# Routed experts of L0_ffn and L3_ffn: token rows sent to the experts and results fetched back by indirect transfers

## The chip, the cores and the metric

One core of one Trainium2 chip runs the whole program. The time is the device time of one execution in microseconds; a median of several executions is given. Smaller is better.

## The reference, cut to what matters

The program is a stack of graph and feed-forward stages on 256 tokens of 768 columns, all in float32. L0_ffn and L3_ffn are mixtures of 8 experts with 2 chosen per token, and a shared expert that takes every token. This is their part of the computation as the kernel does it:

```
probs = softmax(x @ router)            # 8 logits per token; the two largest: w1, w2, divided by w1 + w2
for each expert e, for the tokens that chose it:
    h = silu(x @ gate[e]) * (x @ up[e])      # 768 -> 768 in L0_ffn, 768 -> 384 in L3_ffn
    out = out + weight * (h @ down[e])       # back to 768
out = out + shared expert(x) + the residual rows
```

In L0_ffn the weights are also scaled with a sigmoid gate between routed and shared experts, and L1_gnn follows with a normalization of each row. L3_ffn is the last stage; its rows are the output.

## The kernel before, in words

The program is written engine by engine: `sync_program`, `tensor_program`, `scalar_program`, `vector_program` and `gpsimd_program` call one function per stage, and what stands first in a function is issued first on that engine. Engines meet through semaphores, `mark` to signal and `at` to wait. Nothing reorders.

Weights stream from DRAM on SP's queue through `weight_ring`, five slots of 128 x 4608 float32 (2304 KB). `load` takes the slots in turn and first waits for `unit_free` of the unit that lay there. A gate, up or down matrix of an L0_ffn expert fills a slot each; in L3_ffn gate and up (1152 KB each) share one, and down (1152 KB) has one.

Each expert has 96 places for tokens (`NARROW`), split as 64 and 32 rows. The place of a token is counted on PE and DVE (`slots_pe`, `slots_dve`). If an expert gets more than 96, a flag is set and `taken_branch` runs a slow correction at the stage's end; every engine tests the flag there.

Token rows come to an expert by products. DVE's `select_dve` writes a 0/1 matrix S (256 tokens x 96 places) for each expert, and `pair_dispatch_pe` multiplies the normalized rows `xn_tok` with S for two experts at a time: 12 products, 24 rows of the trace, since the trace shows each float32 product as two. The results come back in the same manner: `weigh_dve` scales S with the token's weight, `weights_turn` turns it on PE, `cb_copy` brings it back, and `combine_A` (64 places of two experts) and `combine_B` (32 places of four) multiply expert outputs `outA`, `outB` with it and add onto banks 0 to 3. Those banks (`acc_tok`) hold the stage's sum from its beginning; `residual_pe` starts them with the residual rows.

Per expert PE does, in L0_ffn (`packed_pe`): gate, up (96 products on 32-column groups), then what `beside_silu_pe` names, the turning of the hidden rows (`packed_hidden_pe`), what `beside_copies_pe` names, and down (48 products). The two `beside` functions put dispatches and combines where ACT and DVE work on the hidden rows. In L3_ffn `both_experts_pe` does the same with half as many products. At the end `shared_down_pe` and the last combines finish the sum; L1_gnn's normalization, or the copies to `x_tok` and the two output transfers, follow.

## Time and profile before

| | |
|---|---|
| median of 3 runs | 1814.47 us (1813.79 to 1817.63) |
| the profiled execution's own time | 1809.26 us |
| its span | 1807.4 us |
| TensorE busy | 1711.3 us, 95% |
| VectorE, ScalarE, GpSimd busy | 624.7, 444.5, 26.4 us |
| mean granted clock | 0.991 |

The span runs from the first to the last instruction; the execution's own time has 1.9 us more around it. Line numbers are those of the kernel before. Matmul lines all have one number, 114, and transposes 117, so work is told by its tiles: `r_xd` is an expert's token rows, `r_hT` its turned hidden rows, `r_S` the selection, `r_cbA` and `r_cbB` the turned weights. L0_ffn's expert loop runs from 555.1 to 741.5 us, L3_ffn's from 1678.0 us to the end.

### The profile page before, as it was taken

How to read it: one execution, taken by the hardware profiler on the slowest of the kernel's cores; microseconds unless marked ns; L12 is line 12 of the kernel's file. 1: busy time of each engine (PE TensorE's matmuls, PEld its weight loads, DVE VectorE, ACT ScalarE, POOL GpSimd, SP SyncE). 2: the span in 40 equal slices, each digit the busy share in tenths (PEclk: the TensorE clock that was granted, in tenths of full speed). 3: DMA queues.
4: the chain of work that ended last, by engine and by line, in shares of the span. 5: the costliest groups of instructions: out<-in, count | busy, mean ns of one | idle time of the engine just before them, and what ended most of it. 6: DMA issues, size and time to landing. Idle time of an engine off the chain costs nothing.

```text
span 1807.4 us, 27462 instructions
## 1 busy us (share of the span) xinstructions
PE 1711.3 (95%) x12188; PEld 1021.6 (57%) x12188; DVE 624.7 (35%) x1178; ACT 444.5 (25%) x816; POOL 26.4 (1%) x35
## 2 busy tenths in 40 slices
PE   7999999999999999799999988887999999999998
PEld 4675445764466555477654433334575645767664
DVE  4415994049972221461420000002422422142331
ACT  0014883048841101341210000002511010131110
POOL 0000000000000000000000000000002000000000
PEclk9999999999999999889999999999999999999999
DMA  9205886139746877402589999999363164301661
GB/s 394 106 26 172 215 251 245 66 109 214 262 163 257 325 301 299 165 1 105 220 346 386 429 429 427 429 427 429 161 260 120 69 249 185 143 27 53 263 248 60
DMA packets 80749, 408.28 MB, mean 226 GB/s; under 512 B 9768, under 2 KB 50240, under 8 KB 58992
## 3 DMA queue, kind: packets, MB, share of 16 engines
q1 hardware_dynamic: 76112, 402.41, 58.6%
q10 hardware_dynamic: 4512, 4.03, 0.7%
q8 instruction: 100, 1.64, 0.4%
q14 instruction: 25, 0.20, 0.0%
HBM read 400.85 MB, written 5.51 MB: 225 GB/s over the span
## 4 chain that ended last, share of the span: by engine, by line
PE 80%; DMA 13%; DVE 4%; ACT 1%; issue 1%; SPq 0%; POOL 0%; DVEq 0%; ACTq 0%
PE banks L114 78%; DMA weight_ring<-in_L_ffn_c_fc_dram 8%; PE banks L117 2%; DMA weight_ring<-in_L_gnn_W_in_dram 2%; DMA weight_ring<-in_L_ffn_c_proj_e_dram 2%; DMA node_parts<-gate_node_parts 1%; DMA gate_rows<-node_parts 1%; DVE stat L273 1%; DVE weight_ring L120 0%; DVE xn_tok L125 0%; DMA ident<-in_c_ident_dram 0%; SPq L154 0%; DMA gate_queries<-in_L_gnn_query_rep_dram 0%; ACT weight_ring L148 0%; DVE xT L137 0%
## 5 line engine op out<-in xcount | busy, mean ns | idle before, releaser
L114 PE MATMUL banks<-weight_ring,xT 128*128 128x384 f32 x864 | 292.5, 490 | 1.5 <-DVE rgat_xr L137 1.5
L120 DVE TENSOR_TENSOR weight_ring<-weight_ring,gate_queries 128x1024 f32<-128x1024 f32 x192 | 222.8, 1222 | 17.5 <-ACT weight_ring L148 11.7
L114 PEld LDWEIGHTS banks<-weight_ring,xT 128*128 128x128 f32 x864 | 161.9, 191 | 107.9 <-issue 7.8
L148 ACT ACTIVATE weight_ring<-banks 128x1024 f32<-128x1024 f32 x192 | 191.0, 1024 | 42.8 <-PE banks L114 39.5
L114 PE MATMUL banks<-xT,weight_ring 128*128 128x256 f32 x792 | 178.2, 379 | 3.2 <-ACT x_tok L151 3.2
L114 PEld LDWEIGHTS banks<-xT,weight_ring 128*128 128x128 f32 x792 | 149.8, 190 | 27.4 <-issue 3.6
L114 PE MATMUL banks<-weight_ring,r_xd 128*32 128x384 f32 (+1 forms) x2304 | 142.7, 406 | 0.0
L114 PE MATMUL banks<-weight_ring,moe_xdT 128*64 128x384 f32 x720 | 122.0, 489 | 20.5 <-DMA weight_ring<-in_L_ffn_c_fc_dram 20.4
L114 PEld LDWEIGHTS banks<-weight_ring,r_xd 128*32 128x32 f32 x2304 | 76.7, 110 | 63.2 <-issue 54.9
L114 PE MATMUL banks<-gate_rows,selrow 96*128 96x512 bf16 x384 | 107.4, 381 | 3.1 <-ACT weight_ring L148 1.8
L114 PE MATMUL banks<-weight_ring,selrow 128*32 128x256 f32 x1536 | 102.0, 385 | 1.6 <-DVE weight_ring L120 1.5
L137 DVE COPY y_tok<-banks 128x384 f32<-128x384 f32 x32 | 17.8, 558 | 247.2 <-PE banks L117 247.2
L114 PEld LDWEIGHTS banks<-weight_ring,moe_xdT 128*64 128x64 f32 x720 | 49.9, 137 | 89.1 <-issue 57.9
L114 PE MATMUL banks<-weight_ring,y_tok 128*64 128x384 f32 x504 | 85.9, 490 | 10.5 <-DMA weight_ring<-in_L_ffn_c_proj_e_dram 10.5
L148 ACT ACTIVATE moe_h_tok<-banks 128x384 f32<-128x384 f32 x32 | 15.7, 491 | 265.9 <-PE banks L114 265.9
L114 PE MATMUL banks<-weight_ring,r_hT 128*32 128x192 f32 (+1 forms) x1152 | 73.2, 407 | 1.0 <-ACT r_hT L151 1.0
L114 PEld LDWEIGHTS banks<-weight_ring,selrow 128*32 128x32 f32 x1536 | 40.4, 109 | 58.2 <-issue 26.7
L114 PEld LDWEIGHTS banks<-weight_ring,y_tok 128*64 128x64 f32 x504 | 34.3, 137 | 55.1 <-issue 39.6
L114 PEld LDWEIGHTS banks<-gate_rows,selrow 96*128 96x128 bf16 x384 | 29.8, 97 | 59.6 <-issue 34.3
L114 PEld LDWEIGHTS banks<-weight_ring,r_hT 128*32 128x32 f32 x1152 | 36.7, 110 | 37.7 <-issue 34.4
L120 DVE TENSOR_TENSOR selrow<-banks,gate_node_parts 128x384 f32<-128x384 f32 x16 | 8.6, 555 | 129.8 <-ACT gate_node_parts L151 99.8
L120 DVE TENSOR_TENSOR r_h<-banks,r_silu 128x256 f32<-128x256 f32 (+2 forms) x32 | 13.3, 416 | 108.9 <-PE banks L114 77.3
(370 smaller groups left out, 1808.1 us busy)
## 6 DMA issues: line engine op xcount, KB each, us to landing
weight_ring<-in_L_ffn_c_fc_dram SPq DMA_DIRECT2D x30, 2304.0 KB, 23.0
weight_ring<-in_L_ffn_c_proj_e_dram SPq DMA_DIRECT2D x21, 2304.0 KB, 28.3
gate_queries<-in_L_gnn_query_rep_dram SPq DMA_DIRECT2D x48, 512.0 KB, 4.4
weight_slot_heads<-in_L_ffn_c_proj_e_dram SPq DMA_DIRECT2D x9, 2304.0 KB, 28.8
weight_ring<-in_L_ffn_w_gate_dram SPq DMA_DIRECT2D x8, 2304.0 KB, 10.0
weight_ring<-in_L_ffn_w_up_dram SPq DMA_DIRECT2D x8, 2304.0 KB, 8.9
weight_ring<-in_L_ffn_w_down_dram SPq DMA_DIRECT2D x8, 2304.0 KB, 9.7
weight_ring<-in_L_ffn_w_dram SPq DMA_DIRECT2D x16, 1152.0 KB, 8.0
```

Of the source, the lines that this page charges most:

```text
L114: return self.e.matmul(out, lhsT, rhs, start=start, stop=stop)
L117: return self.e.transpose(out, src, self.ident[0:n, 0:n])
L120: return self.e.tensor_tensor(out, a, b, op)
L137: return self.e.tensor_copy(out, a)
L148: return self.e.activation(out, a, f, **kw)
L273: t = v.e.bn_stats(half_stats[:, c, h, :], src[:, 2 * c + h, :])
```

## The change

- ACT clears a DRAM table `slot_rows` (768 x 768 float32, 2304 KB) early in L0_gnn, by a transfer from a constant.
- Experts 0 and 1 still get their rows by products. After that DVE (`index_dve`, 11 small operations) makes for each token the row numbers of its two places, and GpSimd (`send_pool`) writes the rows of `xn_tok` to `slot_rows` by four indirect transfers of 128 rows of 3 KB. For experts 2 to 7 SP loads 96 rows from the table (`slot_rows_sp`), and PE turns them with 6 transposes (`rows_turn_pe`); DVE and ACT copy half each (`expert_xd`).
- An expert's output goes by two SP transfers (64 and 32 rows) to a DRAM table `expert_rows` (`expert_rows_sp`). After the last, GpSimd (`fetch_pool`) reads each token's two rows with four indirect transfers into `chosen`, and DVE (`chosen_dve`) adds them with their weights onto `x_tok`. `weigh_dve`, `weights_turn`, `cb_copy` and the combines are gone.
- Banks 0 to 3 hold only the shared expert's sum, made at the end (`last_sums_pe`: 10 products in L0_ffn, 20 in L3_ffn). In L0_ffn `rows_added_pe` then adds `x_tok` with 4 products; in L3_ffn DVE adds the banks to `x_tok`, and `y3` to it in the loop. The 4 residual products at L0_ffn's beginning are gone; of those of L3_ffn two pairs became 3 small idle products each and two pairs are gone.
- PE begins the next expert's gate (in L3_ffn gate and up) before it turns the hidden rows, and finishes it after. Load order follows.
- Several semaphores are renamed; that is left out here.

```diff
+            a.dma(dram["slot_rows"], dram["c_zero"]).then_inc(*mark("slot_rows_zero", 0, 16))
...
+        def index_dve(v, B, v1, v2, z):
+
+            s, slot, mask, oh2, tm, row = B["stage"], B["slot"][:], B["sc"][1][:], *(x[:] for x in B["sc"][2:5])
+            both, second, w1, w2 = (B["pick"][:, i, :] for i in range(4))
+            v.then(v.ts(tm, slot, float(NARROW), ALU.is_ge, float(BEYOND), ALU.mult))
+            v.then(v.stt(row, bc(desc[:].unsqueeze(1), [P, TC, NEXP]), -float(NARROW), slot, ALU.mult, ALU.add))
+            v.then(v.tt(row, row, tm, ALU.add))
+            v.tt(tm, row, mask, ALU.mult)
+            v.then(v.tt(oh2, row, oh2, ALU.mult))
+            v.red(both, tm, ALU.add)
+            v.then(v.red(second, oh2, ALU.add))
+            v.tt(w1, v1, z, ALU.mult)
+            v.tt(w2, v2, z, ALU.mult)
+            v.stt(B["index"][:, 0, :], both, float(SLOTS), second, ALU.add, ALU.subtract)
+            v.ts(B["index"][:, 1, :], second, float(SLOTS), ALU.add).then_inc(*mark("index", s))
+
+        def send_pool(g, B):
+
+            s = B["stage"]
+            g.then(g.e.memset(B["chosen"][:], 0.0))
+            g.wait_ge(*at("slot_rows_zero"))
+            g.wait_ge(*at("index", s))
+            for c in range(TC):
+                for i in range(2):
+                    g.e.indirect_dma_start(
+                        out=dram["slot_rows"], out_offset=bass.IndirectOffsetOnAxis(ap=B["index"][:, i, c:c + 1], axis=0),
+                        in_=xn_tok[:, c, :], in_offset=None, bounds_check=SLOTS - 1, oob_is_err=False,
+                    ).then_inc(*mark("rows_sent", s, 16))
+
+        def fetch_pool(g, B):
+
+            s = B["stage"]
+            g.wait_ge(*at("expert_rows_0", (s, NEXP - 2)))
+            g.wait_ge(*at("expert_rows_1", (s, NEXP - 1)))
+            for c in range(TC):
+                for i in range(2):
+                    g.e.indirect_dma_start(
+                        out=B["chosen"][:, c, i, :], out_offset=None, in_=dram["expert_rows"],
+                        in_offset=bass.IndirectOffsetOnAxis(ap=B["index"][:, i, c:c + 1], axis=0),
+                        bounds_check=SLOTS - 1, oob_is_err=False,
+                    ).then_inc(*mark(f"rows_chosen_{c}", s, 16))
+
+        def chosen_dve(v, B, c):
+
+            s, row = B["stage"], x_tok[:, c, :]
+            v.wait_ge(*at(f"rows_chosen_{c}", s))
+            v.then(v.stt(row, B["chosen"][:, c, 0, :], B["pick"][:, 2, c:c + 1], row, ALU.mult, ALU.add))
+            v.stt(row, B["chosen"][:, c, 1, :], B["pick"][:, 3, c:c + 1], row, ALU.mult, ALU.add
+                  ).then_inc(*mark("rows_added", (s, c)))
+
+        def slot_rows_sp(q, B, e):
+            s = B["stage"]
+            if e < 4:
+                q.wait_ge(*at("rows_sent", s))
+            else:
+                q.wait_ge(*at("rows_turned", (s, e - 2)))
+            q.dma(B["rows"][0:NARROW, e % 2, :], dram["slot_rows"][NARROW * e:NARROW * (e + 1), :]
+                  ).then_inc(*mark(f"slot_rows_{e % 2}", (s, e), 16))
+
+        def expert_rows_sp(q, B, e):
+            s, z, r = B["stage"], e % 2, e % 4
+            wait_expert_out(q, B, e)
+            q.dma(dram["expert_rows"][NARROW * e:NARROW * e + SLOT, :], B["outA"][SLOT * z:SLOT * (z + 1), :]
+                  ).then_inc(*mark(f"expert_rows_{z}", (s, e), 16))
+            q.dma(dram["expert_rows"][NARROW * e + SLOT:NARROW * (e + 1), :], B["outB"][THIRD * r:THIRD * (r + 1), :]
+                  ).then_inc(*mark(f"expert_rows_{z}", (s, e), 16))
 
...
         def L0_ffn_sp(q):
+            last = NEXP - 1
+            load(q, ("L0u", 0), dram["L0_ffn_w_up"][0])
             for e in range(NEXP):
-                if e:
-                    load(q, ("L0g", e), dram["L0_ffn_w_gate"][e])
-                load(q, ("L0u", e), dram["L0_ffn_w_up"][e])
-                load(q, ("L0d", e), dram["L0_ffn_w_down"][e])
+                if e < last:
+                    load(q, ("L0g", e + 1), dram["L0_ffn_w_gate"][e + 1])
+                    if e >= 2:
+                        expert_rows_sp(q, R0, e - 2)
+                if e < last - 1:
+                    load(q, ("L0d", e), dram["L0_ffn_w_down"][e])
+                    load(q, ("L0u", e + 1), dram["L0_ffn_w_up"][e + 1])
+                    if e == 0:
+                        slot_rows_sp(q, R0, 2)
+                        slot_rows_sp(q, R0, 3)
+                    elif e < 5:
+                        slot_rows_sp(q, R0, e + 3)
+            load(q, ("L0u", last), dram["L0_ffn_w_up"][last])
+            load(q, ("L0d", last - 1), dram["L0_ffn_w_down"][last - 1])
+            load(q, ("L0d", last), dram["L0_ffn_w_down"][last])
+            expert_rows_sp(q, R0, last - 2)
             load(q, "L0sd", dram["L0_ffn_ws_down"])
+            expert_rows_sp(q, R0, last - 1)
+            expert_rows_sp(q, R0, last)
             taken_branch(q, R0, over_sp)
 
...
+            last = NEXP - 1
+            load(q, ("L3gu", 0), dram["L3_ffn_Weg"][0], dram["L3_ffn_Weu"][0])
             for e in range(NEXP):
-                load(q, ("L3gu", e), dram["L3_ffn_Weg"][e], dram["L3_ffn_Weu"][e])
+                if e < last:
+                    load(q, ("L3gu", e + 1), dram["L3_ffn_Weg"][e + 1], dram["L3_ffn_Weu"][e + 1])
+                    if e >= 3:
+                        expert_rows_sp(q, R3, e - 3)
                 load(q, ("L3d", e), dram["L3_ffn_Wed"][e])
+                if e == 1:
+                    slot_rows_sp(q, R3, 2)
+                    slot_rows_sp(q, R3, 3)
+                elif 1 < e < 6:
+                    slot_rows_sp(q, R3, e + 2)
+            expert_rows_sp(q, R3, last - 3)
             load(q, "L3sd", dram["L3_ffn_Wsd"])
+            expert_rows_sp(q, R3, last - 2)
+            expert_rows_sp(q, R3, last - 1)
+            expert_rows_sp(q, R3, last)
             taken_branch(q, R3, over_sp)
 
         def L3_ffn_pe(pe):
...
-            both_dve(v, R3)
+            both_dve(v, R3, v1, v2, z)
             taken_branch(v, R3, over_dve)
-            v.wait_ge(*at("unit_free", "L3sd"))
-            v.cp(as_tok(x_tok[:])[:, 2:4, :], acc_tok[:, 2:4, :]).then_inc(*mark("rows", "out"))
+            for c in range(TC):
+                row = as_tok(x_tok[:])[:, 2 * c:2 * c + 2, :]
+                v.wait_ge(*at("rows_added", ("r3", c)))
+                v.wait_ge(*(at("unit_free", "L3sd") if c else at("projected", "L3sd")))
```

New functions of PE and the loop of `packed_pe` as it is after the change:

```python
        def rows_turn_pe(pe, B, e):
            s = B["stage"]
            pe.wait_ge(*at(f"slot_rows_{e % 2}", (s, e)))
            wait_xd(pe, B, e - 1)
            for f in range(DC):
                t = pe.tr(PS[:, 1 + f // 3, f % 3 * NARROW:(f % 3 + 1) * NARROW],
                          B["rows"][0:NARROW, e % 2, f * P:(f + 1) * P], NARROW)
            t.then_inc(*mark("rows_turned", (s, e)))
...
        def last_sums_pe(pe, B, done):
            hc, down_u = B["shared"][1], B["shared"][4]
            for c in range(TC):
                for o in range(done if c == 0 else 0, hc):
                    t = shared_down_pe(pe, B["shared"], c, o, hc == DC)
                t.then_inc(*(mark("unit_free", down_u) if c else mark("projected", down_u)))
...
        def rows_added_pe(pe, B, c):
            s = B["stage"]
            pe.wait_ge(*at("rows_added", (s, c)))
            for h in range(2):
                t = pe.mm(PS[:, 2 * c + h, 0:HALF], ident[:], x_tok[:, c, h * HALF:(h + 1) * HALF], False, True)
            t.then_inc(*mark("rows_summed", (s, c)))
...
        def packed_pe(pe, B):
...
            gate_wide_pe(pe, B, 0)
            pe.wait_ge(*at("shared_h", (key, 2)))
            gate_narrow_pe(pe, B, 0)
            pe.wait_ge(*at("row_copied", ("L0_ffn", "spread")))
            up_pe(pe, B, 0)
            for e in range(NEXP):
                if e < last:
                    gate_wide_pe(pe, B, e + 1)
                packed_hidden_pe(pe, B, e)
                if e == 0:
                    worst_turn_pe(pe, B)
                elif e == 1:
                    pe.wait_ge(*at("flag", s))
                if e + 2 < NEXP:
                    rows_turn_pe(pe, B, e + 2)
                if e < last:
                    gate_narrow_pe(pe, B, e + 1)
                if e == last - 1:
                    up_pe(pe, B, e + 1)
                elif e == last:
                    wait_expert_out(pe, B, e - 1)
                    shared_down_pe(pe, B["shared"], 0, 0, False)
                down_pe(pe, B, e)
                if e < last - 1:
                    up_pe(pe, B, e + 1)
            last_sums_pe(pe, B, 1)
            for c in range(TC):
                rows_added_pe(pe, B, c)

```

In L3_ffn `both_experts_pe` has the same loop with `both_wide_pe` and `both_narrow_pe` in place of the gate's two parts, no `up_pe`, and two outputs of the shared sum for the first 128 tokens ahead of the last down.

PE's order for expert 3 of L0_ffn before (r_SA, r_S: weights and selection; r_h: hidden rows):

```order
L114 MATMUL banks<-weight_ring,r_xd 32x384 x24
L114 MATMUL banks<-weight_ring,r_xd 32x192 x24
L114 MATMUL banks<-weight_ring,r_xd 32x384 x24
L114 MATMUL banks<-weight_ring,r_xd 32x192 x24
L117 MATMUL banks<-ident,r_SA 128x128 x2
L114 MATMUL banks<-r_S,xn_tok 128x192 x4
L117 MATMUL banks<-ident,r_h 128x128 x3
L114 MATMUL banks<-ident,r_h 64x64 x2
L117 MATMUL banks<-ident,r_h 128x128
L114 MATMUL banks<-r_S,xn_tok 128x192 x8
L114 MATMUL banks<-weight_ring,r_hT 32x384 x24
L114 MATMUL banks<-weight_ring,r_hT 32x192 x24
```

And PE's order in one turn of the changed loop (r_rows: the 96 rows loaded from the table):

```order
L117 MATMUL banks<-weight_ring,r_xd 32x384 x24
L120 MATMUL banks<-ident,r_h 128x128 x3
L117 MATMUL banks<-ident,r_h 64x64 x2
L120 MATMUL banks<-ident,r_h 128x128
L120 MATMUL banks<-ident,r_rows 128x96 x6
L117 MATMUL banks<-weight_ring,r_xd 32x192 x24
L117 MATMUL banks<-weight_ring,r_hT 32x384 x24
L117 MATMUL banks<-weight_ring,r_hT 32x192 x24
L117 MATMUL banks<-weight_ring,r_xd 32x384 x24
L117 MATMUL banks<-weight_ring,r_xd 32x192 x24
```

The dispatch and the turned weights are gone, six transposes are new, and 24 products of the next expert stand ahead of the turning of the hidden rows.

SP's queue in the changed L0_ffn, from expert 0's down weights on, with what each waits for:

```order
L157 DMA weight_ring<-in_L_ffn_w_down_dram 128x4608
L157 DMA weight_ring<-in_L_ffn_w_up_dram 128x4608 [waits unit_free]
L157 DMA r_rows<-slot_rows 96x768 [waits rows_sent]
L157 DMA r_rows<-slot_rows 96x768
L157 DMA weight_ring<-in_L_ffn_w_gate_dram 128x4608 [waits unit_free]
L157 DMA weight_ring<-in_L_ffn_w_down_dram 128x4608 [waits unit_free]
L157 DMA weight_ring<-in_L_ffn_w_up_dram 128x4608 [waits unit_free]
L157 DMA r_rows<-slot_rows 96x768 [waits rows_turned]
L157 DMA weight_ring<-in_L_ffn_w_gate_dram 128x4608 [waits unit_free]
L157 DMA expert_rows<-r_outA 64x768 [waits expert_out_act,expert_out_dve]
L157 DMA expert_rows<-r_outB 32x768
```

Weight loads alone stood here before; now SP also waits for the sent rows, for turned rows and for outputs, with weight loads queued behind.

## Rows read from the trace of the kernel before

**Rows 1.** The page: size, and the chain that ended last, by engine.
```profile
span 1807.4 us, 27462 instructions
...
PE 80%; DMA 13%; DVE 4%; ACT 1%; issue 1%; SPq 0%; POOL 0%; DVEq 0%; ACTq 0%
```

**Rows 2.** Stretches: length, busy PE, PEld, DVE, ACT, POOL, clock, DMA share, GB/s.
```profile
642.00:665.00 23.00, 23.00 (x304) 12.27 (x300) 3.81 (x12) 2.12 (x5) 0.00 (x0) 1.00 0.79 310
1730.00:1745.00 15.00, 15.00 (x193) 7.99 (x189) 3.79 (x13) 1.82 (x5) 0.00 (x0) 1.00 0.62 238
555.00:575.00 20.00, 19.25 (x302) 10.74 (x305) 5.10 (x20) 1.98 (x6) 0.00 (x0) 1.00 0.92 355
1000.00:1200.00 200.00, 171.41 (x1017) 72.20 (x1015) 13.39 (x24) 9.34 (x19) 0.00 (x0) 1.00 1.01 428
745.00:750.00 5.00, 0.48 (x2) 0.39 (x2) 1.35 (x2) 0.80 (x1) 0.01 (x1) 0.50 0.92 376
```

**Rows 3.** Timeline, start of L0_ffn: start, us, engine, line, work, idle before.
```profile
530.58 2.83 PE L114 MATMUL banks<-x_tok,ident 128*128 128x384 f32 x8
...
536.11 1.06 PE L114 MATMUL banks<-r_route,before 128*128 128x8 f32 x8
...
568.89 6.03 PE L114 MATMUL banks<-weight_ring,r_hT 128*32 128x384 f32 x96 [0.61 <-ACT r_hT L151]
```

**Rows 4.** Timeline, PE inside expert 3 of L0_ffn.
```profile
630.65 0.44 PE L117 MATMUL banks<-ident,r_SA 128*128 128x128 f32 x2
...
630.92 1.47 PE L114 MATMUL banks<-r_S,xn_tok 128*128 128x192 f32 x8
...
633.08 2.77 PE L114 MATMUL banks<-r_S,xn_tok 128*128 128x192 f32 x16
...
635.77 6.03 PE L114 MATMUL banks<-weight_ring,r_hT 128*32 128x384 f32 x96
```

**Rows 5.** Timeline, end of L0_ffn and the step to L1_gnn.
```profile
733.50 2.85 PE L114 MATMUL banks<-weight_ring,shared_h 128*128 128x384 f32 x8
...
736.19 2.74 PE L114 MATMUL banks<-r_outA,r_cbA 128*128 128x384 f32 x8
...
738.77 2.74 PE L114 MATMUL banks<-r_outB,r_cbB 128*128 128x384 f32 x8
...
741.55 1.03 DVE L273 BATCH_NORM_STATS2 stat<-banks 128x6 f32<-128x384 f32 x2 [7.56 <-PE banks L114]
...
742.61 0.30 PE L114 MATMUL banks<-small 64*64 64x24 f32 x4 [1.10 <-issue]
...
749.52 1.01 PE L114 MATMUL banks<-before,ident 128*128 128x256 f32 x2 [6.61 <-issue]
```

**Rows 6.** Timeline, start of L3_ffn.
```profile
1633.85 0.87 PE L117 MATMUL banks<-ident,xn_tok 128*128 128x128 f32 x6 [0.86 <-DVE xn_tok L124]
...
1641.67 1.06 PE L114 MATMUL banks<-r_route,before 128*128 128x8 f32 x8 [1.74 <-DVE r_route L120]
...
1643.05 1.05 DVE L125 TENSOR_SCALAR r_S<-iota_slot,r_slots,r_route 128x96 f32<-128x96 f32 x4
...
1647.85 4.06 PE L114 MATMUL banks<-r_S,xn_tok 128*128 128x192 f32 x24
```

**Rows 7.** Timeline, end of L3_ffn and of the program.
```profile
1792.20 5.43 PE L114 MATMUL banks<-weight_ring,shared_h 128*128 128x384 f32 x16
...
1802.82 0.96 DVE L137 COPY x_tok<-banks 128x768 f32<-128x768 f32 x1 [9.50 <-PE banks L114]
1803.64 0.82 SPq L154 DMA_DIRECT2D out_dram<-x_tok  x2
```

**Rows 8.** Timeline, the same small size on DVE and on POOL.
```profile
742.86 0.15 DVE L124 TENSOR_SCALAR stat<-stat 128x1 f32<-128x1 f32 x1
...
743.09 0.55 POOL L120 TENSOR_TENSOR stat<-stat 128x1 f32<-128x1 f32 x1 [1.09 <-DVE stat L124]
```

**Rows 9.** DMA issues: count, KB each, median us from issue to landing.
```profile
weight_ring<-in_L_ffn_w_gate_dram SPq DMA_DIRECT2D x8, 2304.0 KB, 10.0
...
node_parts<-gate_node_parts SPq DMA_DIRECT2D x4, 576.0 KB, 6.0
...
out_dram<-x_tok SPq DMA_DIRECT2D x2, 384.0 KB, 2.7
```

More of the change, by code:

```diff
@@ L1384, in pair_xd @@
+            last_sums_pe(pe, B, 1)
+            for c in range(TC):
+                rows_added_pe(pe, B, c)
+        def pair_xd(lane, B, i, engine):
             s, weight = B["stage"], B["weight"]
-            lane.wait_ge(*at("pair_sent", (s, p, i)))
+            lane.wait_ge(*at("pair_sent", (s, i)))
             o = B["xd"][:, :, 2 * i:2 * i + 2, :].rearrange("p e k s -> p k e s")
-            src = PS[:, sent_bank(B, i), 0:4 * NARROW].rearrange("p (k e s) -> p k e s", k=2, e=2)
+            src = PS[:, 1 + i, 0:4 * NARROW].rearrange("p (k e s) -> p k e s", k=2, e=2)
+            if weight is None:
+                t = lane.copy(o, src) if engine == "act" else lane.cp(o, src)
+            else:
+                for k in range(2):
+                    if engine == "act":
+                        t = lane.act(o[:, k, :, :], src[:, k, :, :], ACT.Copy, scale=weight[:, 2 * i + k:2 * i + k + 1])
+                    else:
+                        t = lane.ts(o[:, k, :, :], src[:, k, :, :], weight[:, 2 * i + k:2 * i + k + 1], ALU.mult)
+            t.then_inc(*mark("xd_" + engine, (s, i and 1)))
@@ L1388, in pair_xd, with expert_xd @@
+        def expert_xd(lane, B, e, engine):
+            s, weight = B["stage"], B["weight"]
+            i = 1 if engine == "act" else 0
+            own = slice(3 * i, 3 * i + 3)
+            lane.wait_ge(*at("rows_turned", (s, e)))
+            o = B["xd"][:, e % 2, own, :]
+            src = PS[:, 1 + i, 0:3 * NARROW].rearrange("p (k s) -> p k s", k=3)
             if weight is None:
@@ new lines, in both_experts_pe, with both_dve @@
+                if e + 2 < NEXP:
+                    rows_turn_pe(pe, B, e + 2)
+                if e < last:
+                    both_narrow_pe(pe, B, e + 1)
+                if e:
+                    wait_expert_out(pe, B, e - 1)
+                if e == last:
+                    for o in range(2):
+                        shared_down_pe(pe, B["shared"], 0, o, False)
+                down_pe(pe, B, e)
+            last_sums_pe(pe, B, 2)
+        def both_dve(v, B, v1, v2, z):
+            s, h, silu, last = B["stage"], B["h"], B["silu"], NEXP - 1
+            first_pair_dve(v, B, v1, v2, z)
@@ L1585, in both_dve @@
                      ALU.mult).then_inc(*mark("routed_h", (s, e, 1)))
-                if e % 2 and e + 1 < NEXP:
-                    pair_xd(v, B, e // 2 + 1, 0, "dve")
-                    pair_xd(v, B, e // 2 + 1, 2, "dve")
+            overflow_dve_worst(v, B)
+            inner_rows(0)
+            for e in range(NEXP):
+                if e + 2 < NEXP:
+                    expert_xd(v, B, e + 2, "dve")
                 if e == 0:
                     overflow_dve_flag(v, B)
+                elif e == 1:
+                    v.tt(x_tok[:], x_tok[:], y3[:], ALU.add)
+                if e < last:
+                    inner_rows(e + 1)
@@ L2077, in L1_gnn_dve @@
         def L1_gnn_dve(v):
[L2078 removed]
+            for c in range(TC):
+                v.wait_ge(*at("rows_summed", ("r0", c)))
+                variance_dve(v, "L1_gnn", c, acc_tok, 1e-5)
+                rows_dve(v, "L1_gnn", c, as_tok(xn_tok[:]), acc_tok)
             tok_to_T_dve(v, "L1_gnn")
@@ L3476, in L3_ffn_dve @@
             slots_dve(v, "L3_ffn", R3["slot"][:], 4)
-            both_dve(v, R3)
+            both_dve(v, R3, v1, v2, z)
             taken_branch(v, R3, over_dve)
-            v.wait_ge(*at("unit_free", "L3sd"))
-            v.cp(as_tok(x_tok[:])[:, 2:4, :], acc_tok[:, 2:4, :]).then_inc(*mark("rows", "out"))
+            for c in range(TC):
+                row = as_tok(x_tok[:])[:, 2 * c:2 * c + 2, :]
+                v.wait_ge(*at("rows_added", ("r3", c)))
+                v.wait_ge(*(at("unit_free", "L3sd") if c else at("projected", "L3sd")))
+                v.tt(row, acc_tok[:, 2 * c:2 * c + 2, :], row, ALU.add).then_inc(*mark("rows", ("out", c)))
         def sync_program(q):
@@ L3490, in sync_program @@
             L3_ffn_sp(q)
-            q.wait_ge(*at("kept", "out"))
-            q.dma(out_dram[:, 0, :], x_tok[:, 0, :]).then_inc(*mark("stored", 0, 16))
-            q.wait_ge(*at("rows", "out"))
-            q.dma(out_dram[:, 1, :], x_tok[:, 1, :]).then_inc(*mark("stored", 0, 16))
+            for c in range(TC):
+                q.wait_ge(*at("rows", ("out", c)))
+                q.dma(out_dram[:, c, :], x_tok[:, c, :]).then_inc(*mark("stored", 0, 16))
             q.wait_ge(*at("stored"))
@@ L3679 @@
         dram[n] = nc.dram_tensor(n, (*tokens, 3, D), BF16, kind="Internal").ap()
+    for n in ("slot_rows", "expert_rows"):
+        dram[n] = nc.dram_tensor(n, (SLOTS, D), F32, kind="Internal").ap()
     build(nc, dram, out)
```

534 lines of the change are left out of this document (239 added, 295 removed).

## The prediction

> **What bounds the kernel now.** I read the page first. Its chain that ended last is 80% PE and 13% DMA [rows 1], so the program waits for PE nearly everywhere, and for weights in one place. The table of stretches shows where. In both loops that the change rewrites PE is busy all the time, while weights come at 310 and 238 GB/s, with the DMA engines busy 0.79 and 0.62 of it [rows 2]. From 1000 to 1200 us (L1_ffn) it is the other way round, with 428 GB/s at a full share [rows 2]. So whatever PE is spared in these two loops is spared the program, as long as transfers keep up and the ends of the stages don't grow. The timelines then give the price of each step and what hides it.
>
> **L0_ffn, what goes.** At the beginning four residual products go, 2.83 us as listed [rows 3]. The mask for the places arrives at 536.1 us [rows 3] whatever PE does, but the up products of the shared expert take the room ahead of it, so all is gained: 2.7 us (entries in a row overlap by some 0.15 us, so I count from start to start). The first turning of weights adds 0.3: 3.0 in all. A dispatch costs 1.3 and 2.7 us (from 633.08 to 635.77) [rows 4]; three of the four pairs lose it, 12.0 us. The turned weights of the later pairs cost 0.27 us, and twice 0.5 with the second matrix [rows 4], 1.2 us. A combine of four products costs 2.58 us (736.19 to 738.77) [rows 5] and a little more where it is cut in two; four of A and two of B make 16.0 us. The wait of 0.61 us for the turned hidden rows of expert 0 [rows 3] is covered by the next expert's products. Sum: 3.0 + 12.0 + 1.2 + 16.0 + 0.6 = 32.8 us.
>
> **L0_ffn, what comes.** Six times six transposes of 96 rows. Six of 128 rows take 0.87 us alone [rows 6]; in the stream I take 0.6 each time, 3.6 us (bounds 2.4 and 5.2). Four products that add x_tok at the end: 2.6 us. A wait for the copies of expert 6 before the shared sum goes on: 0.5. So without any wait for the fetched rows PE ends at 741.4 - 32.8 + 6.7 = 715.3 us. Of this the ten shared products (6.5 us) and x_tok's four stand behind the last down, which therefore ends at 706.2. The 11 small DVE operations for the tables and the copies of turned rows cost nothing: DVE and ACT are busy 3.8 and 2.1 of 23 us [rows 2] and lose the work on weights; without that cover the copies of an expert would cost about 1 us each. POOL clears `chosen` while it has nothing else to do.
>
> **The end of L0_ffn** is a new chain, and no row shows an indirect transfer. Copies of expert 7: 0.4, to 706.6. SP issues two transfers at 0.41 each (two took 0.82 [rows 7]): 707.4. They land in 2.7 us, as 384 KB to DRAM does [rows 9]: 710.1. Then POOL. Its smallest operation takes 0.55 us where DVE takes 0.15 [rows 8], so I take an issue by POOL at 0.41 x 3.7 = 1.5 us, an estimate. Two issues and 2.7 us to land: the first 128 tokens are there at 715.8, the others at 718.8. DVE needs two passes of 0.96 [rows 7] for each: 720.8. Two products: PE ends at 722.1. The gain is 741.4 - 722.1 = **19.3 us**. Bounds of the four fetches, instead of 8.7 us: 2.7 (one landing, issues free [rows 9]) and 24 (four in a row, each at the 6.0 us of a 576 KB write [rows 9]). I take the value near the lower one because 384 KB out and 1.5 MB in four pieces are near that row. What follows is unchanged: the test of the flag costs PE 1.10 us and then it stands 6.61 us [rows 5] while DVE normalizes; both count from PE's last product. In that stand the granted clock falls to 0.50 [rows 2], the 1.2 GHz level; a longer wait before it may bring that forward by a microsecond or two, which is left to the range.
>
> In the Trainium skill, DMA: Bandwidth & Descriptors (Anatomy of one DMA), a transfer from GpSimd takes 2.0 us + bytes / 436 GB/s; by that page each fetch of 384 KB would take 2.9 us, an estimate, close to the 2.7 of the row, and no run here shows it.
>
> **L3_ffn.** Dispatch starts at 1647.85 [rows 6]. Now gate and up of the shared expert stand before the places, which they delay by 0.7 us, since the mask comes at 1641.67 [rows 6]; the selection, done at 1644.1 [rows 6], then comes at 1644.9, and dispatch with it: 2.9 gained, and 0.3 for the first turning. The loop loses the same three dispatches (12.3), turns (1.2), six combines (16.2) and a wait of 0.6, and gets 3.6 of transposes and 0.5 of waiting: 26.2. The residual products lay in waits or before the mask and are worth nothing more. PE's last product moves from 1802.6 to 1802.6 - 3.2 - 26.2 = 1773.2. The last 20 products (eight take 5.3 [rows 7]) are 13.3 us, so the last down ends at 1759.9. The same chain: copies 1760.5, issues 1761.3, landed 1764.0, first rows 1769.7, second 1772.7, DVE 1774.7. PE is just done, so this chain decides. Then DVE tests the flag. PE's row gives 1.1 for the test alone and 7.7 with its stand [rows 5]; DVE has only two instructions left, so I take 2.0, and 0 and 7.7 as bounds. Two sums of 0.96 [rows 7]: 1778.7. From DVE's end to the end of the span there are 3.6 us (1803.78 to 1807.4 [rows 7]): 1782.3. Gain **25.1 us**.
>
> **Elsewhere.** Clearing the table moves 2304 KB on ACT's queue early in L0_gnn, beside small loads that PE needs. A load of this size lands in 10.0 us [rows 9]; I take 1 us, bounds 0 and 10. Expert 2's rows must be there at about 569 us. The tables are ready near 548, four sends and one landing at the prices above take 8.7 and SP's loads 5: slack of some 7 us. In L3_ffn, where two weight loads are queued ahead, the slack is 2 us; SP's weight loads behind these waits are due 20 us later. Weight ring: order of loads and of frees agree, and outputs are awaited when they are just done.
>
> Sum: 19.3 + 25.1 - 1 = 43.4 us. The profiled execution's own time, 1809.26, becomes 1765.9. The three runs have a median 5.2 us above it; I put the forecast between the two bases, nearer the profile: **1768 us**.
>
> **Rivals.**
> 1. *Transfers bound the loops.* An expert of L0_ffn keeps 11.65 us of gate and up, 5.85 of down (635.77 to 641.62), 0.85 of turning (about 632.2 to 633.08) [rows 4] and gets 0.6: 18.95 us instead of about 23, for 7.08 MB of weights and now 0.59 MB of rows, 405 GB/s. In L3_ffn, with half the products, it is 10.3 us for 4.13 MB, 401 GB/s. For it: the busiest stretch of L0_ffn gave 355 GB/s at a share of 0.92, and 310 at 0.79 extrapolates to 392. Against it: 428 GB/s were reached [rows 2], and the ring leads by 20 us. At 355 an expert takes 21.6 us, six times 2.65 more, less what the lead absorbs, and L3_ffn adds 3: 12 us, **1780 us**. In the Trainium skill, DMA: Bandwidth & Descriptors (Specifications), HBM gives a core about 358 GB/s; by that an expert would take 21.4 us, an estimate of the same size, which speaks against this change. The 428 GB/s over 200 us disagree with that limit, hence a chance of 0.15.
> 2. *The fetches go one by one*, 24 us for the four: L0_ffn gains 4, L3_ffn 9.8, less 1: **1799 us**. For it: one engine issues them. Against: nothing in the program makes one wait for another. 0.07. The Trainium skill's SBUF — State Buffer (the "DVE blocks DMA" trap) says that some DVE copies keep GpSimd from writing its descriptors; here DVE idles during the fetches, so it would touch the sends alone.
> 3. *Slower.* The fetches queue behind weights. After expert 7's outputs SP at once issues four 2304 KB loads for L1_ffn, and such a load lands in 10.0 us [rows 9]. With 10 us for each fetch, 40 in all, in both stages, L0_ffn loses 12 and L3_ffn 6.2: slower by 19 us, **1830 us**. By the sums above the gain is 60.8 us less twice the fetch time (four fetches of a stage together), so it turns at 30.4 us, 7.6 per transfer. Against: L3_ffn has no loads at its end. 0.05.
> 4. *L1_ffn eats L0_ffn's gain.* It runs at the full DMA rate [rows 2]; if its stream did not start earlier, 18.3 us would go: **1787 us**. Against: its loads wait for slots that PE frees, and these move with PE. 0.08.
>
> **How the numbers follow.** Forecast 0.65, rivals 0.15, 0.07, 0.05, 0.08. With every fetch landed in 2.7 us (6 us in each stage), less for the flag and more from runs near the profile's base, 1754 is the low end. With rivals 1 and 4 the high end is 1790, which leaves out rivals 2 and 3. A measurement can tell about 0.2%, 3.6 us. Slower only by rival 3: 0.05; within 0.2%: 0.01; faster: 0.94.
>
> **What would show it.** One turn of L0_ffn's loop in 19.0 us and of L3_ffn's in 10.3, with no DMA as releaser; `r_rows` transposes at 0.6 us without a wait; the last down near 706 and PE's last addition near 722; fetches landing 3 to 9 us after POOL is released; the span near 1764. PE or PEld waiting for `weight_ring` is rival 1; more than 20 us between `expert_rows` and DVE's passes is rival 2 or 3; an L1_ffn that ends when it did is rival 4. A wait at expert 2 for `r_rows` would show that I mis-sized the sends.

## The result, and the profile after

The changed kernel takes 1783.91 us (median of 4 runs, 1780.23 to 1788.35), the kernel before on the same chip 1815.43 (4 runs, 1813.79 to 1817.63). The ratio is 0.983, with a 95% interval from 0.9814 to 0.9847: 31.5 us faster. Forecast was a gain of 43 to 47, to 1768 us, within 1754 to 1790. The time is in the range, but 16 us above the forecast, and where these went is the subject of what follows.

The page of the changed kernel, beside [rows 1]: size, the software queue's packets, MB and share, and the chain.

```profile
span 1783.3 us, 27162 instructions
...
q0 software_dynamic: 1280, 6.29, 1.0%
...
PE 77%; DMA 16%; DVE 4%; issue 1%; ACT 1%; SPq 0%; POOL 0%; DVEq 0%; POOLq 0%; ACTq 0%
```

PE's share of the chain fell by 3 points, and DMA's rose by 3. The two loops are not where DMA entered. Beside [rows 2], the same stretches inside the loops (length, busy PE, PEld, DVE, ACT, POOL, clock, DMA share, GB/s):

```profile
642.00:665.00 23.00, 23.00 (x382) 12.74 (x374) 3.87 (x9) 2.55 (x6) 0.00 (x0) 1.00 1.01 395
1730.00:1745.00 15.00, 15.00 (x273) 8.57 (x267) 4.08 (x11) 3.25 (x11) 0.00 (x0) 1.00 0.99 375
```

The DMA engines are now full, and PE still never waits. The timeline of PE shows one turn of each loop, beside [rows 4], from the first product of a gate to the next one, and the transposes of the fetched-back rows:

```profile
620.50 9.87 PE L117 MATMUL banks<-weight_ring,r_xd 128*32 128x384 f32 x144
...
631.21 0.66 PE L120 MATMUL banks<-ident,r_rows 96*128 96x96 f32 x6
...
639.59 9.87 PE L117 MATMUL banks<-weight_ring,r_xd 128*32 128x384 f32 x144
...
1687.42 0.71 PE L120 MATMUL banks<-ident,r_rows 96*128 96x96 f32 x6 [0.78 <-DMA r_rows<-slot_rows]
...
1692.95 4.05 PE L117 MATMUL banks<-weight_ring,r_xd 128*32 128x384 f32 x48
...
1703.30 4.05 PE L117 MATMUL banks<-weight_ring,r_xd 128*32 128x384 f32 x48
```

A turn of L0_ffn's loop takes 19.09 us (18.95 forecast), one of L3_ffn's 10.35 (10.3 forecast). One of the rows' loads is late, by 0.8 us, at expert 2 of L3_ffn. The end of L0_ffn is another matter. Timeline of the changed kernel there, by engine: SP's issues, POOL's fetches, DVE's sums, PE's last additions.

```profile
711.63 0.58 SPq L157 DMA_DIRECT2D expert_rows<-r_outB  x1
713.79 1.31 SPq L157 DMA_DIRECT2D weight_ring<-in_L_ffn_c_attn_w_dram  x3
715.15 0.52 SPq L157 DMA_DIRECT2D weight_ring<-in_L_ffn_c_proj_w_dram  x1
717.31 0.33 SPq L157 DMA_DIRECT2D weight_ring<-in_L_ffn_c_fc_dram  x1
...
715.27 1.05 POOL L1212 DMA_INDIRECT r_chosen<-expert_rows,r_index  x1 [158.43 <-DMA expert_rows<-r_outB]
...
719.25 1.00 POOL L1212 DMA_INDIRECT r_chosen<-expert_rows,r_index  x1 [0.30 <-issue]
...
728.12 2.07 DVE L134 SCALAR_TENSOR_TENSOR x_tok<-r_chosen,r_pick,x_tok 128x768 f32<-128x768 f32 x2 [17.07 <-DMA r_chosen<-expert_rows,r_index]
736.28 2.07 DVE L134 SCALAR_TENSOR_TENSOR x_tok<-r_chosen,r_pick,x_tok 128x768 f32<-128x768 f32 x2 [6.08 <-DMA r_chosen<-expert_rows,r_index]
...
730.25 2.93 PE L117 MATMUL banks<-x_tok,ident 128*128 128x384 f32 x4 [12.97 <-DVE x_tok L134]
738.40 2.93 PE L117 MATMUL banks<-x_tok,ident 128*128 128x384 f32 x4 [5.23 <-DVE x_tok L134]
```

Three weight loads are issued 1.5 us ahead of the first fetch, and two more beside the fetches. DVE gets the first pair of rows 12.9 us after the first fetch was issued and the second pair 21.0 us after it; 5.7 and 8.7 had been reckoned. PE's last addition ends at 741.3, where its last product ended at 741.5 before. The same chain at the end of L3_ffn, where no weights are left to load:

```profile
1762.91 0.58 SPq L157 DMA_DIRECT2D expert_rows<-r_outB  x1
...
1767.41 1.05 POOL L1212 DMA_INDIRECT r_chosen<-expert_rows,r_index  x1 [109.44 <-DMA expert_rows<-r_outB]
...
1774.22 4.05 DVE L134 SCALAR_TENSOR_TENSOR x_tok<-r_chosen,r_pick,x_tok 128x768 f32<-128x768 f32 x4 [11.83 <-DMA r_chosen<-expert_rows,r_index]
1778.53 1.82 DVE L123 TENSOR_TENSOR x_tok<-banks,x_tok 128x768 f32<-128x768 f32 x2 [0.25 <-DVE x_tok L134]
1779.52 1.22 SPq L157 DMA_DIRECT2D out_dram<-x_tok  x2
```

There DVE starts 6.8 us after the first issue and meets no second wait. From the first issue to the end of DVE's sums it is 23.1 us in L0_ffn and 10.9 us here, so the same four fetches cost 12 us less where nothing competes. That, and the granted clock, gave the two questions.

To compare profiles stage by stage I use marks that both kernels have, on POOL: the first normalization of L0_ffn (523.12 before), the memset of `gat_vec` that opens L1's first stage (741.57), the memset of `rgat_vecT` that opens L2's (1242.11), and the cast of `sw_bias` (1359.70). Of L3_ffn it is the normalization of the second 128 tokens (1632.19). Changed kernels have two more, the first send and the first fetch.

### The profile page after: what moved, and what is told of

The parts are those of the page before. It is cut to its first block, busy times and chain, and to the rows that moved or that the text cites. A ratio compares the mean times of both kernels' runs of the same rounds, so it can differ in the third digit from the quotient of the medians.

```text
span 1783.3 us, 27162 instructions
## 1 busy us (share of the span) xinstructions
PE 1669.1 (94%) x11992; PEld 987.5 (55%) x11992; DVE 617.0 (35%) x1116; ACT 442.6 (25%) x818; POOL 47.8 (3%) x53
## 4 chain that ended last, share of the span: by engine, by line
PE 77%; DMA 16%; DVE 4%; issue 1%; ACT 1%; SPq 0%; POOL 0%; DVEq 0%; POOLq 0%; ACTq 0%
PE banks L117 74%; DMA weight_ring<-in_L_ffn_c_fc_dram 8%; PE banks L120 3%; DMA weight_ring<-in_L_ffn_c_proj_e_dram 2%; DMA weight_ring<-in_L_gnn_W_in_dram 2%; DMA r_chosen<-expert_rows,r_index 1%; DVE weight_ring L123 1%; DMA gate_queries<-in_L_gnn_query_rep_dram 1%; DMA node_parts<-gate_node_parts 1%; DMA r_rows<-slot_rows 1%; DVE stat L276 1%; DMA gate_rows<-node_parts 1%; SPq L157 0%; DVE x_tok L134 0%; DMA expert_rows<-r_outB 0%
## 5 line engine op out<-in xcount | busy, mean ns | idle before, releaser
L151 ACT ACTIVATE r_silu<-banks 128x256 f32<-128x256 f32 (+2 forms) x32 | 12.1, 377 | 122.6 <-PE banks L117 122.6
```

The source lines that it names most:

```text
L151: return self.e.activation(out, a, f, **kw)
```

## Experiment 1: the changed kernel again

Nothing is edited.

> The changed kernel once more, nothing edited. Chance theory: the 3 us of low clock at 531 to 538 us (granted clock 0.5 in 533:536), the 5 us lost at 1244 to 1292 us (clock 0.72 in 1240:1260 where the kernel before had 0.91) and the later end of L0_gnn are different from run to run, so at least one of the three differs in this profile by over 2 us. Cause theory: the change sets them, by its order of work before those places, and all three stand within 0.5 us of where they stood: normalization of L1's x at 738 to 743, gate_rows' third wait at 286, 24 first products in 8.1 us. Time 1780 to 1788 either way.

Measured: 1783.28 us (5 runs; before 1815.63, 9 runs), ratio 0.9818 (0.9805 to 0.9832). Its profile differs from the first in two of the three places. The normalization of L0_ffn starts at 523.1 (525.1 in the first), and L2's first stretch takes 117.0 us (122.2). The beginning of L0_ffn, from normalization to first send, takes 26.7 us both times. The end of L0_ffn repeats to 0.15 us: 23.3 us from the first fetch to the memset (23.1). So the end is the kernel's own; the rest needed more profiles.

## Experiments 2 and 3: weights held until the rows are fetched

```
 def L1_ffn_sp(q):
+    q.wait_ge(*at("rows_chosen_1", "r0"))
     for i in range(3):
         load(q, ("c_attn", i), dram["L1_ffn_c_attn_w"][i])
```

> SP issues the five weight loads of L1_ffn only after the fourth fetch of L0_ffn has landed. Queue theory: the fetches were late because 11.5 MB of weights were given to the same DMA engines 1.5 us ahead of them; alone they land as in L3_ffn, where the first pair's sum began 4.5 us after the second issue ended, so DVE adds from 722 and PE's last addition ends near 730 in place of 741.3; c_attn then lands from 727 to 739, ahead of its first use near 740: about 11 us faster, 1773. Rival, the fetches' own latency in this place (96 KB pieces written 3 us before, 128 descriptors each): DVE starts at 728 and 736 as before, and the late weights cost 5 to 15 us more: 1789 to 1799.

Experiment 3 also issues the first of these loads ahead of expert 6's rows:

```
     load(q, "L0sd", dram["L0_ffn_ws_down"])
+    load(q, ("c_attn", 0), dram["L1_ffn_c_attn_w"][0])
     expert_rows_sp(q, R0, last - 1)
...
 def L1_ffn_sp(q):
-    for i in range(3):
+    q.wait_ge(*at("rows_chosen_1", "r0"))
+    for i in range(1, 3):
```

> As e1_hold, and the first of the three c_attn loads goes ahead of expert 6's rows on SP, into the stretch 693 to 713 us in which the DMA engines were 20% busy. Queue theory: 11 us faster than the changed kernel, and if c_attn's landing is the next thing late in e1_hold, up to 5 us more; if it is not, the same as e1_hold within 1 us. Rival as in e1_hold.

Measured: 1770.97 us (ratio 0.9765, 0.9745 to 0.9785) and 1769.62 us (0.9752, 0.9739 to 0.9766), 12 and 14 us faster than the changed kernel beside them. The timeline of e1_hold at the end of L0_ffn:

```profile
715.40 1.05 POOL L1212 DMA_INDIRECT r_chosen<-expert_rows,r_index  x1 [158.42 <-DMA expert_rows<-r_outB]
...
721.41 2.07 DVE L134 SCALAR_TENSOR_TENSOR x_tok<-r_chosen,r_pick,x_tok 128x768 f32<-128x768 f32 x2 [10.22 <-DMA r_chosen<-expert_rows,r_index]
723.74 2.07 DVE L134 SCALAR_TENSOR_TENSOR x_tok<-r_chosen,r_pick,x_tok 128x768 f32<-128x768 f32 x2 [0.26 <-DMA r_chosen<-expert_rows,r_index]
...
723.53 5.49 PE L117 MATMUL banks<-x_tok,ident 128*128 128x384 f32 x8 [6.12 <-DVE x_tok L134]
...
723.74 1.31 SPq L157 DMA_DIRECT2D weight_ring<-in_L_ffn_c_attn_w_dram  x3
```

The first pair is there after 6.0 us in place of 12.9, and the second by 8.3 in place of 21.0. From the first fetch to the memset it is 10.5 us in both experiments, 12.7 less than with the weights. The fetches' own latency is refuted as the cause. The late weights cost nothing that can be told from the spread: from the memset to L2's it was 499.0 us in e1_hold and 504.1 in e2_early_hold, 501.0 to 503.1 in four profiles of kernels that hold no load, and 498.7 to 502.0 in three of the kernel before. e2_early_hold, with one of the loads issued 33 us before the others, gains no more from the first fetch to the memset.

Landings say the same. In experiment 1, whose trace has all four, a fetch landed 8.6, 11.6, 14.0 and 17.1 us after its own issue; in e1_hold it took 4.0 to 4.6 us. For a single fetch 4.2 had been reckoned, 1.5 for the issue and 2.7 to land.

## Experiments 4, 5 and 6: which weights, and why

Experiment 4 holds four of the five loads, experiment 5 two of them (`c_proj` and `c_fc`):

```
 for i in range(3):                          # e4_one_ahead
+    if i == 1:
+        q.wait_ge(*at("rows_chosen_1", "r0"))
     load(q, ("c_attn", i), dram["L1_ffn_c_attn_w"][i])
+q.wait_ge(*at("rows_chosen_1", "r0"))       # e5_three_ahead, alone
 load(q, "c_proj", dram["L1_ffn_c_proj_w"])
```

> Of L1_ffn's five weight loads one (c_attn 0) goes ahead of the fetches as in the changed kernel, four wait until the fetches have landed. Measured so far, from POOL's first fetch issue to its memset for L1_ffn: 23.1 to 23.3 us with all five loads ahead, 10.5 us with none. Line theory (the fetches are served after all the weights issued before them) and turns theory (the DMA engines take a packet of the one queue and a packet of the other in turn; weight packets are large, fetch packets small) both say little: one load is 5.4 us of traffic at 428 GB/s and began 1.5 us ahead: 11 to 14 us. A fixed price for any weight load in flight would give 23.

> The three c_attn loads go ahead of the fetches, c_proj and c_fc wait for them. Line theory: 3 loads are 16.2 us of traffic from 713.8, so the first pair lands after 730 and both pairs together by 732; from first issue to the memset 19 to 20 us, and DVE's two sums stand one right behind the other. Turns theory: the first pair lands as in the changed kernel, where DVE began 12.9 us after the first issue, and the second finds little of the weights left, 3 to 4 us later instead of 8.2: 17 to 19 us to the memset, with a wait of 1 to 2 us between the sums.

Experiment 6 holds nothing, but cuts the five loads into six transfers each, so that a partition's 18 KB go as six pieces of 3 KB:

```
-load(q, ("c_attn", i), dram["L1_ffn_c_attn_w"][i])
+load(q, ("c_attn", i), *(dram["L1_ffn_c_attn_w"][i][:, k * D:(k + 1) * D]
+                         for k in range(DC)))
...                                          # c_proj and the first c_fc in the same way
```

> The order of the changed kernel, with all five loads ahead, but each is issued as six transfers of 768 columns, so that a weight packet is 3 KB in place of 18 KB; bytes the same. Turns theory: the fetches' packets of 3 KB then get about half of each engine, so the first pair lands some 5 us after its issue in place of 10.5 and the memset comes 12 to 14 us after the first issue in place of 23.1: 9 to 11 us faster than the changed kernel. Line theory: the bytes ahead are the same, so 22 to 24 us and the time of the changed kernel, 1783. Bytes shared evenly between the queues whatever the packets: no change either.

| kernel | loads beside the fetches | first pair at | second pair at | first fetch to memset | median us (runs) | ratio (95%) |
|---|---|---|---|---|---|---|
| changed, twice | 5 | 12.9 | 21.0 | 23.1, 23.3 | 1783.3 (5) | 0.9818 (0.9805 to 0.9832) |
| e5_three_ahead | 3 | 12.8 | 20.9 | 23.1 | 1782.5 (4) | 0.9838 (0.9801 to 0.9875) |
| e6_small_pieces | 5, small packets | 8.6 | 11.7 | 13.8 | 1774.3 (4) | 0.9786 (0.9749 to 0.9823) |
| e4_one_ahead | 1 | 8.7 | 10.6 | 12.8 | 1772.1 (4) | 0.9772 (0.9743 to 0.9801) |
| e1_hold | 0 | 6.0 | 8.3 | 10.5 | 1771.0 (5) | 0.9765 (0.9745 to 0.9785) |

All times but the medians are us from the first fetch's issue in the profile, worked out as above. In e4_one_ahead the second pair landed while DVE still added the first; its time is that at which SP, which waits for both pairs, went on. The loads of experiments 7 and 8 below are those of the changed kernel and of experiment 3, and they repeat the figures: 12.9, 21.1 and 23.2 us, and 6.1, 8.5 and 10.7. Experiments 4 to 6 and 8 ran beside 7 runs of the kernel before with a median of 1816.32 us, the others beside 9 with 1815.63. The rows behind the second line, e5_three_ahead's timeline:

```profile
710.23 1.05 POOL L1212 DMA_INDIRECT r_chosen<-expert_rows,r_index  x1 [158.44 <-DMA expert_rows<-r_outB]
...
722.99 2.07 DVE L134 SCALAR_TENSOR_TENSOR x_tok<-r_chosen,r_pick,x_tok 128x768 f32<-128x768 f32 x2 [17.00 <-DMA r_chosen<-expert_rows,r_index]
731.17 2.07 DVE L134 SCALAR_TENSOR_TENSOR x_tok<-r_chosen,r_pick,x_tok 128x768 f32<-128x768 f32 x2 [6.11 <-DMA r_chosen<-expert_rows,r_index]
```

and behind the third, e6_small_pieces':

```profile
709.82 1.06 POOL L1212 DMA_INDIRECT r_chosen<-expert_rows,r_index  x1 [158.44 <-DMA expert_rows<-r_outB]
...
718.43 2.07 DVE L134 SCALAR_TENSOR_TENSOR x_tok<-r_chosen,r_pick,x_tok 128x768 f32<-128x768 f32 x2 [12.85 <-DMA r_chosen<-expert_rows,r_index]
721.49 2.07 DVE L134 SCALAR_TENSOR_TENSOR x_tok<-r_chosen,r_pick,x_tok 128x768 f32<-128x768 f32 x2 [0.99 <-DMA r_chosen<-expert_rows,r_index]
```

With small packets 9.3 us come back, where the expectation gave a strict line, and a sharing by bytes, nothing. The time alone would not decide, since the edit also changes the pace: SP issues the pieces one by one, and when POOL issued its first fetch 4 of them (1.6 MB) stood ahead, in place of three whole loads (7.1 MB). The packets decide. The DMA queues of the two kernels from 713 to 735 us, first the changed one (packets, MB, share of 16 engines; q1 carries SP's loads, q0 POOL's fetches):

```profile
q1 hardware_dynamic: 472, 6.89, 77.7%
q0 software_dynamic: 305, 1.57, 17.3%
```

and e6_small_pieces:

```profile
q1 hardware_dynamic: 2578, 7.05, 82.8%
q0 software_dynamic: 320, 1.57, 18.0%
```

And 2 us in which both queues move, 723 to 725 us of the changed kernel,

```profile
q1 hardware_dynamic: 33, 0.61, 70.7%
q0 software_dynamic: 35, 0.20, 23.5%
```

and 718 to 720 us of e6_small_pieces:

```profile
q0 software_dynamic: 108, 0.55, 66.4%
q1 hardware_dynamic: 104, 0.27, 34.1%
```

In both kernels it goes packet for packet, 35 to 33 and 108 to 104, whatever the sizes. A strict line would have let the fetches pass only behind the three loads issued ahead of them; but the second of these landed at 730.0 us, when DVE had had the first pair since 728.1. A sharing by bytes would have given the fetches half of the bytes, and in the changed kernel they got a quarter. The Trainium skill's DMA: Bandwidth & Descriptors (Queues, rings and completion order) has this rule: each engine takes turns between the queues that have work, a whole packet at a time. By that rule it is the packet size of the other queue that counts, and the traces agree, with the counts above.

What the turns cost: the four fetches are 320 packets with 4.9 KB in the mean, so a pair is 10 on each of 16 engines. A weight packet is a partition's 18 KB (2304 KB in 128); at 428 GB/s over 16 engines it holds an engine for 0.69 us. If each fetch packet waits for one of them, a pair comes 10 x 0.69 = 6.9 us later and both 13.8, an estimate. Measured: 12.9 - 6.0 = 6.9 for the first pair, and 12.7 for both. That the first pair fits so well is luck, because a second delay is in it: the first fetch packet moves 1.8 us after the first issue in e1_hold, and 4.0 to 4.4 us after it in every kernel with loads ahead. That is 2.3 to 2.6 us more, with small packets too (4.0 in e6_small_pieces), so turns don't explain it, and its cause stays open. With packets of 3 KB the turns alone give 1.1 us a pair, 2.3 in all; measured were 2.6 for the first pair and 3.3 for both (13.8 - 10.5), most of it the later start. So turns with 18 KB packets account for some 10 of the 12.7 us, and the later start for some 2.5.

On e5_three_ahead the expectation was wrong: three loads delayed both pairs as much as five. The line theory had both pairs together by then, and they came 8.2 us apart. The turns theory stands, its working was bad. Three loads are 24 weight packets for each engine, the 20 fetch packets of both pairs need 20 of these, and the 1.5 to 4 us by which the loads lead use up 2 to 6 more, an estimate; that is about all of the 24, so nothing was left to save. One load is 8 packets, of which part had passed, and it cost 12.8 - 10.5 = 2.3 us, no more than the later start (4.2 us in place of 1.8).

## Experiments 7 to 10: the clearing of the table, and the clock

The forecast had 1 us for the clearing of the table, which runs near 116 us. Experiment 7 moves it to a stretch in which DMA is idle, before `relu_act(a, 1)`; experiment 8 joins it with experiment 3.

```
-    a.dma(dram["slot_rows"], dram["c_zero"]).then_inc(*mark("slot_rows_zero", 0, 16))
     for n in range(NQ):
         query_split_act(a, n)
...
+    a.dma(dram["slot_rows"], dram["c_zero"]).then_inc(*mark("slot_rows_zero", 0, 16))
     relu_act(a, 1)
```

> The clearing of the table (2304 KB) is issued near 345 us, where DMA stands idle to 375, in place of 116 us. Contention theory: the clearing pushed L0_gnn's first loop late by its 2304 KB of traffic; PE's first transposes of L0_ffn start at 525.5 as in the kernel before, not at 527.4: 2 us faster, 1782. Rival, chance or code of its own: it stays at 527.4 and the time is the same.

> e2_early_hold and e3_clear_late together: the candidate for the fastest. The edits touch different stretches; the first is worth 12.7 us in the stage, the second was worth nothing that stood out. 1767 to 1771; were the clearing's traffic a cost after all, 2 us under e2_early_hold's 1769.6.

Measured: 1783.09 us (5 runs, ratio 0.9818, 0.9798 to 0.9837), no other than the changed kernel's 1783.28; and 1769.75 us (4 runs, 0.9758, 0.9729 to 0.9786), no other than e2_early_hold's 1769.62. The length of L0_gnn, from POOL's first normalization to that of L0_ffn, was 513.0 to 517.2 us in seven profiles with the early clearing, 514.5 and 515.3 with the late one, and 514.7, 515.1 and 517.8 in three of the kernel before. The clearing costs nothing that can be told from this spread. The contention theory for it falls.

Two profiles of the kernel before, unedited, were to show whether the clock drop near 533 us comes with the change:

> The kernel before once more, nothing edited. Measured so far on nine profiles of changed kernels: from the first normalization of L0_ffn to the first send 23.7, 25.0 or 26.7 us, by the clock granted from 531 to 538, a stretch that begins ahead of the first instruction of PE that the change moved. Chance theory: the kernel before meets the same drop in some executions, so this profile or the next shows the clock under 1.0 between 530 and 545 us, or L2's first stretch (first memset of rgat_vecT to the cast of sw_bias) away from the 117.6 us of its first profile by over 2 us. Cause theory: both are as in its first profile, 1.00 and 117.6.

> The same again, as in c1_before: chance theory says that at least one of the two profiles shows a clock under 1.0 between 530 and 545 us or L2's first stretch away from 117.6 us by over 2 us; cause theory says neither does.

Measured: 1817.77 and 1813.35 us, one run each. Both show the drop: c1_before, where it began earlier, has 0.77 from 531 to 538 us, and the other 0.50 from 533 to 539; L2's first stretch took 122.8 us in the one and 117.0 in the other. One stretch in three kernels (columns as above); first the changed kernel,

```profile
533.00:539.00 6.00, 6.00 (x16) 4.89 (x17) 4.35 (x26) 1.59 (x3) 0.00 (x0) 0.53 0.99 403
```

then c2_before, the kernel before in another execution,

```profile
533.00:539.00 6.00, 6.00 (x16) 3.88 (x16) 3.46 (x20) 1.59 (x3) 0.00 (x0) 0.50 0.95 395
```

and e2_early_hold, whose code here is that of the changed kernel:

```profile
533.00:539.00 6.00, 6.00 (x31) 5.06 (x30) 4.08 (x24) 1.60 (x3) 0.00 (x0) 1.00 1.00 412
```

Near 0.50 PE runs at the 1.2 GHz level, and does 16 products in the 6 us in which it does 31 at 2.4 GHz. PE had waited twice in the 6 us before, 0.4 us for the normalized rows and 0.6 us for xT, in each of these three profiles, and in one of them the clock stayed up. From normalization to first send the changed kernels took 26.7 us in four profiles, 25.0 in three and 23.7 in two, with a mean clock from 526 to 545 us of 0.82, 0.91 and 1.00, so the drop costs up to 3.0 us. It comes to either kernel: in the three profiles of the kernel before, the first product of expert 0 came 32.0, 33.3 and 35.0 us after the normalization.

## Why the prediction came out as it did

The profiled executions. Gains by stretch, in us:

| stretch | before | after | gain | forecast |
|---|---|---|---|---|
| L0_gnn | 514.7 | 516.8 | -2.1 | -1 |
| L0_ffn, to the memset | 218.5 | 213.3 | 5.2 | 19.3 |
| L1, to L2's memset | 500.5 | 501.0 | -0.4 | 0 |
| L2's first stretch | 117.6 | 122.2 | -4.7 | 0 |
| from there to L3_ffn's norm | 272.5 | 271.5 | 1.0 | 0 |
| L3_ffn | 175.2 | 150.2 | 25.1 | 25.1 |

- *L0_ffn, what goes and comes: right.* In e2_early_hold, with the clock up and no weights beside the fetches, the stage took 197.7 us, 20.8 less than before; 19.3 was forecast. The front gave 2.8 of its 3.0: the first product of expert 0 came 29.2 us after the normalization there, 32.0 before. Turning six experts' rows cost 0.66 each; 0.6 was taken.
- *The end of L0_ffn: the step that failed.* The last down ends at 710.6, or 705.6 without the late start (2.0) and the low clock (3.0), and POOL's first fetch at 715.3 is 710.3 in the same way; 706.2 and 710.1 had been reckoned. Then came "two issues and 2.7 us to land: the first 128 tokens are there at 715.8". The row behind that price, a write of the output at the end of the program, has an empty DMA system around it, as L3_ffn's end has. With it L3_ffn and e1_hold agree: rows after 6.0 to 6.8 us, both pairs by 8.3, against 5.7 and 8.7. So the term for the landing was mis-sized in L0_ffn alone, because it left out the weights: four fetches beside weight packets, 12.7 us more. The sends at the beginning of L0_ffn met the same: SP's loads of the sent rows could be issued only at 564.35, 7.5 us after POOL's last send had ended (556.84), where 2.7 had been reckoned, but the slack hid it and PE did not wait.
- *Rival 3* named this mechanism and its place ("the fetches queue behind weights") but joined both stages, took it for a line at 10 us a fetch, and got 0.05. It belonged into the sum for L0_ffn: SP's loads are issued right there in the program, ahead of the fetches. Its argument against, that L3_ffn has no loads at its end, was right and held for L3_ffn only.
- *L3_ffn: 25.1 us forecast, 25.1 measured, in part by luck.* Reckoned and measured, in us after the normalization: last down 127.7 and 128.1, first fetch 131.8 and 134.3, DVE's first sum 137.5 and 141.1, its sums of the banks 144.5 and 145.4, end 150.1 and 150.2. Copies, issues and landings took 3 us longer; DVE's test of the flag shows as 0.25 us where 2.0 was taken, DVE met no second wait, and the end was 0.7 us shorter. In nine profiles of changed kernels the stage took 149.9 to 152.2 us, against 175.2 in all three of the kernel before, so the gain is 23.0 to 25.3 us. In five of the nine (e1_hold and e4_one_ahead to e7_both_moved) the clock fell to the 1.2 GHz level near its beginning (0.91 in the mean over 20 us in e1_hold, 1.00 in the first profile of the changed kernel), and the first product of expert 0 came 44.2 us after the normalization in place of 42.6; whether the change brings that about stays open. The slack of 2 us for expert 2's rows was too large, since PE waits 0.8 us there.
- *Rival 1, transfers bound the loops: refuted.* 395 and 375 GB/s with a full share, and PE busy throughout. It was near.
- *Rival 2, fetches one by one: refuted.* 8.3 us for all four when alone.
- *Rival 4: refuted.* L1 kept its length, 501.0 against 500.5 us, and began 3.2 us earlier.
- *The base.* With the 12.7 us the forecast of 43.4 becomes 30.7, and 31.5 were measured in the medians. The first profile pair alone shows 24.1, since the kernel before had been caught with the clock up in the front of L0_ffn and in L2. Its own time was 1809.3 where its median was 1815; the forecast was put nearer to that profile than to the medians, which made it 4 us too low. So of the 16 us that the result lies above the forecast, 12.7 are the weights beside the fetches and most of the rest is the base; that it lies within the range at all is owed to the width given to rivals 1 and 4, and neither came.

**The fastest version** by its median is e2_early_hold, 1769.62 us (1769.37 to 1773.73), with e7_both_moved, e1_hold and e4_one_ahead within its spread. It is 14 us faster than the changed kernel and 46 faster than the kernel before.

## What to carry to other kernels

Where a change puts a new transfer at the end of a stage, look at what the other queues are given at that moment; a landing time taken from a quiet stretch is then only the lower bound. What a transfer of small rows pays beside bulk loads went here by its number of packets times the time of one packet of the other queue, and some 2.5 us for a later start, so hold the bulk loads until it has landed, or cut them into small packets. And take more than one profile before a few microseconds are read from a difference between two: L2's first stretch differed by 5 us in the same code.

## What the runs showed of the hardware

An indirect transfer of 128 rows of 3 KB costs POOL 0.97 to 1.19 us and 0.3 between two; with the DMA engines free the rows are in use 3.6 us after the issue of a pair ended (717.8 to 721.4 in e1_hold). Cutting 2304 KB loads into six cost SP 0.46 us a transfer at first (9 in 4.2 us) and 0.74 in the mean (18 in 13.4 us), and the DMA engines little: 399 GB/s from 722 to 735 us, against 427 with whole loads. Two queues with work moved packet for packet (35 to 33, and 108 to 104). After the same two short waits of PE near 530 us the granted clock fell to the 1.2 GHz level in nine of twelve profiles and stayed at the 2.4 GHz level in three; what decides it was not found.
